# A graph layer kernel: the rows of x turned by DMA from their f16 halves, the combination of x and mean as f16 products, and the masked maximum in passes of 1024 columns

## What is computed

```python
mask = (adj > 0)
deg  = sum(mask, axis=1)
agg  = mask @ x / max(deg, 1)
out0 = relu(concat([x @ W_self + b_self, agg @ W_nb + b_nb]) @ W_comb + b_comb)
x    = layernorm(x + out0)

neib_att = tanh(neigh @ Wn1 + bn1) @ Wn2 + bn2
value    = neigh @ Wv + bv
x_att    = tanh(x @ Wx1 + bx1) @ Wx2 + bx2
ws   = leaky_relu(x_att @ neib_att.T)             # 4096x4096
ws   = softmax(where(adj > 0, ws, -9e15), axis=1)
out1 = concat([x @ Wfx + bfx, ws @ value])
x    = layernorm(x + out1)
```

## Time and profile before

| what | value |
|---|---|
| median of three runs | 768.94 us |
| the profiled execution: its own time | 770.73 us |
| its span | 768.9 us |
| PE busy | 733.2 us (95%) |
| weight loads (PEld) busy | 631.0 us (82%) |
| DVE busy | 610.5 us (79%) |
| ACT busy | 584.7 us (76%) |
| POOL busy | 125.3 us (16%) |
| granted TensorE clock | 0.996 of full |
| DMA issue to landing, mask turn of 128x1024 in bf16 | 4.2 us median |

### The profile page before, as it was taken

One profiled execution on the slowest core, in us unless ns is written; L12 is line 12 of the kernel. 1 busy time (PEld: TensorE's weight loads), 2 busy tenths in 40 slices (PEclk: granted clock), 3 DMA queues, 4 the chain that ended last, 5 costly groups with the idle time before them and its releaser, 6 DMA issues.

```text
span 768.9 us, 20264 instructions
## 1 busy us (share of the span) xinstructions
PE 733.2 (95%) x7536; PEld 631.0 (82%) x7536; DVE 610.5 (79%) x1563; ACT 584.7 (76%) x1078; POOL 125.3 (16%) x241
## 2 busy tenths in 40 slices
PE   5989989999999999999999999999999999999785
PEld 4646768888888888888888889888888888887564
DVE  4886477888888888888888888888888888877874
ACT  2455258888888888888888888888888888888995
POOL 0010120111111111111111111111111111111101
PEclk9999999999999999999999999999999999999999
DMA  8968997876677776676876668677667677620000
GB/s 266 363 151 163 220 246 172 179 173 148 157 150 175 176 180 158 158 156 161 180 179 150 160 164 159 167 180 172 138 171 163 170 179 174 122 43 8 8 9 14
DMA packets 175154, 120.43 MB, mean 157 GB/s; under 512 B 140368, under 2 KB 158672, under 8 KB 175056
## 3 DMA queue, kind: packets, MB, share of 16 engines
q1 hardware_dynamic: 174612, 119.11, 65.1%
q10 hardware_dynamic: 444, 0.02, 0.0%
HBM read 81.35 MB, written 4.19 MB: 111 GB/s over the span
## 4 chain that ended last, share of the span: by engine, by line
PE 87%; ACT 4%; DVE 3%; issue 3%; DMA 1%; POOL 1%; SPq 0%; POOLq 0%; ACTq 0%; DVEq 0%
PE ps_v L1036 20%; PE ps_t L1023 14%; PE ps_agg L999 14%; PE ps_agg L1002 14%; PE ps_agg L1056 7%; PE ps_s L1014 6%; PE ps_v L921 2%; PE ps_s L913 2%; PE ps_x L1073 1%; PE ps_x L1076 1%; ACT score L829 1%; DMA neigh_sb<-in_L_gnn_neigh_dram 1%; ACT score L822 1%; PE ps_x L930 1%; PE ps_t L904 1%
## 5 line engine op out<-in xcount | busy, mean ns | idle before, releaser
L999 PE MATMUL ps_agg<-x,mask_t 128*128 128x257 f16 x1024 | 239.7, 272 | 1.5 <-DMA mask_t<-mask 1.5
L1002 PE MATMUL ps_agg<-x,mask_t 128*128 128x256 f16 x1024 | 234.5, 272 | 0.0
L679 DVE TENSOR_TENSOR late<-ps_t,late 128x512 f16<-128x512 f32 x256 | 174.8, 683 | 74.2 <-ACT late L835 71.6
L1036 PEld LDWEIGHTS ps_v<-v,late 128*128 128x128 f16 x3072 | 189.9, 97 | 50.9 <-DVE late L679 16.6
L1036 PE MATMUL ps_v<-v,late 128*128 128x128 f16 x3072 | 213.5, 219 | 9.2 <-DVE late L679 6.7
L822 ACT ACTIVATE score<-ps_s,sc 128x512 f32<-128x512 f32 x256 | 178.0, 695 | 53.0 <-PE ps_s L1014 51.5
L622 DVE CUSTOM_DVE_ANT_0 score<-score,mask 128x512 f32<-128x512 f32 x256 | 176.2, 688 | 18.7 <-ACT score L822 17.2
L835 ACT CAST late<-ps_t 128x512 f16<-128x512 f32 x256 | 150.2, 587 | 15.2 <-PE ps_t L1023 15.1
L1023 PE MATMUL ps_t<-ident,score 128*128 128x128 f32 x1024 | 157.3, 276 | 3.4 <-ACT score L829 3.4
L829 ACT ACTIVATE score<-score,exp_bias,sc 128x1024 f32<-128x1024 f32 x128 | 158.7, 1240 | 1.6 <-DVE exp_bias L631 1.6
L1023 PEld LDWEIGHTS ps_t<-ident,score 128*128 128x128 f32 x1024 | 107.9, 141 | 6.8 <-ACT score L829 4.7
(11 more groups left out here) (125 smaller groups left out, 705.7 us busy)
## 6 DMA issues: line engine op xcount, KB each, us to landing
adj_sb<-in_adj_dram SPq DMA_DIRECT2D x128, 512.0 KB, 4.7
neigh_sb<-in_L_gnn_neigh_dram SPq DMA_DIRECT2D x8, 512.0 KB, 8.0
score<-in_x_dram SPq DMA_DIRECT2D x8, 512.0 KB, 8.5
x_in<-in_x_dram SPq DMA_DIRECT2D x32, 128.0 KB, 3.9
out_dram<-out_sb SPq DMA_DIRECT2D x32, 128.0 KB, 4.5
mask_t<-mask SPq DMA_TRANSPOSE x128, 4.2
mask<-in_L_gnn_W_comb_dram SPq DMA_DIRECT2D x1, 512.0 KB, 10.1
mask<-in_L_gnn_W_self_dram SPq DMA_DIRECT2D x1, 256.0 KB, 7.1
```

What stands on the lines that cost most here:

```text
L679: dve.tensor_tensor(p_lo[:, k % 2, :], ps_t[k % 2][:, :], p_hi[:, k % 2, :], ALU.subtract).then_inc(p_lo_made, 1)
L999: mm = pe.matmul(agg[:, 0:D + 1], mask_t8[:, c, 0, :], x16[:, c, 0:D + 1], start=(c == 0), stop=(c == NC - 1), skip_group_check=True)
L1002: mm = pe.matmul(agg[:, 0:D], mask_t8[:, c, 0, :], x16[:, c, X_LO:X_LO + D], start=False, stop=False, skip_group_check=True)
L1036: mm = pe.matmul(ps_v[:, 0:DV], p[:, k % 2, chunk], v16[:, c, v:v + DV], start=(c == 0 and part == 0), stop=(c == NC - 1 and part == 2))
```

## The change

The rows of x are no longer turned by PE out of a float32 load. SP turns the 512 columns of f16 halves of a block (`turn_x`, in slot 4 of the block) by a DMA transpose into `x_t`; PE's slot 9 keeps the two transposes of the mean. The turned mean is split: ACT makes the high half (slot 10, 256 columns instead of 512), DVE the low half (`mean_low`, slot 11). `m_both` is scaled and split into `m16` in the preparation (a bound over `m_both`, two more ACT and two more DVE instructions in slots 6 and 7, and a third column in the all-reduce on POOL). The combination is twelve f16 products of 256 columns. Layer 0 scales its input on the way. All stages from the combination on stand one slot later, so the loop has one slot more. The masked maximum goes over 1024 columns at a time, in every second slot, and two quarters of the mask are made one slot later.

```diff
-MASK_SLOTS = (-6, -5, -2, -1)
+MASK_SLOTS = (-6, -4, -2, 0)
 MEAN_AT = 8
 MEAN_T_AT = 9
-MEAN_COPY_AT = 10
-COMBINE_AT = 11
...
+MEAN_SPLIT_AT = 10
+MEAN_LOW_AT = 11
+X_TURN_AT = 4
+COMBINE_AT = 12
...
+            def turn_x(b):
+                sp.wait_ge(x_lo_made, b // TR + 1)
+                at_least(sp, combined, b - 1)
+                sp.dma_start_transpose(x_t[:, b % 2, :, :], x16[:, b, 0:2 * D]).then_inc(x_t_in[b % 2], 16)
...
+            def m_low(c):
+                dve.wait_ge(m_hi_made, c + 1)
+                dve.scalar_tensor_tensor(out=m16[:, 1, c, :], in0=m_both[:, c, :], scalar=m_scale, in1=m16[:, 0, c, :],
+                                         op0=ALU.mult, op1=ALU.subtract).then_inc(m_split, 1)
...
-            def masked_scores(b, k):
-                dve.wait_ge(leaky_made, NG * b + k + 1)
-                dve.wait_ge(mask_made, NQ * b + k // 2 + 1)
-                part = slice(k * GW, (k + 1) * GW)
+            def masked_scores(b, q):
+                dve.wait_ge(leaky_made, NG * b + 2 * q + 2)
+                dve.wait_ge(mask_made, NQ * b + q + 1)
+                part = slice(q * QW, (q + 1) * QW)
...
+            def mean_low(b):
+                dve.wait_ge(mean_hi_made, b + 1)
+                dve.scalar_tensor_tensor(out=mean_t[:, 1, :], in0=ps_agg[b % 2][:, 0:D], scalar=x_scale,
+                                         in1=mean_t[:, 0, :], op0=ALU.mult, op1=ALU.subtract).then_inc(mean_lo_made, 1)
...
-                if d := due(s, SCORE_AT + 1):
-                    masked_scores(*d)
+                if (d := due(s, SCORE_AT + 2)) and d[1] % 2 == 0:
+                    masked_scores(d[0], d[1] // 2)
+                if d := due(s, MEAN_LOW_AT, 0):
+                    mean_low(d[0])
...
-            def mean_x_t_copy(b):
+            def mean_high(b):
...
-                act.copy(mean_x_t[:, :], ps_agg[b % 2][:, :]).then_inc(mean_x_t_copied, 1)
+                act.activation(mean_t[:, 0, :], ps_agg[b % 2][:, 0:D], ACT.Copy, scale=x_scale).then_inc(mean_hi_made, 1)
...
             def mean_transpose(b):
                 pe.wait_ge(mean_made, b + 1)
-                pe.wait_ge(x_in_in[b % 2], 16 * (b // 2 + 1))
                 for dc in range(DC):
-                    pe.transpose(ps_agg[b % 2][:, dc * P:(dc + 1) * P], mean[:, dc * P:(dc + 1) * P], ident[:, :])
-                for dc in range(DC):
-                    mm = pe.transpose(ps_agg[b % 2][:, D + dc * P:D + (dc + 1) * P],
-                                      x_in[:, b % 2, dc * P:(dc + 1) * P], ident[:, :])
...
             def combine(b):
...
+                pe.wait_ge(x_t_in[b % 2], 16 * (b // 2 + 1))
+                pe.wait_ge(mean_lo_made, b + 1)
+                for k, ((r, w), dc) in enumerate(product(HI_LO, range(DC))):
+                    pe.matmul(ps_agg[b % 2][:, 0:D], x_t[:, b % 2, (1 - r) * DC + dc, :], m16[:, w, dc, D:2 * D],
+                              start=(k == 0), stop=False)
+                for k, ((r, w), dc) in enumerate(product(HI_LO, range(DC))):
+                    mm = pe.matmul(ps_agg[b % 2][:, 0:D], mean_t[:, r, dc * P:(dc + 1) * P], m16[:, w, dc, 0:D],
+                                   start=False, stop=(k == 3 * DC - 1))
```

More of the change, by code:

```diff
@@ L48 @@
 RES_BUFS = 4
-MASK_SLOTS = (-6, -5, -2, -1)
+MASK_SLOTS = (-6, -4, -2, 0)
 MEAN_AT = 8
 MEAN_T_AT = 9
-MEAN_COPY_AT = 10
-COMBINE_AT = 11
[L57 to L70, removed]
+MEAN_SPLIT_AT = 10
+MEAN_LOW_AT = 11
+X_TURN_AT = 4
+COMBINE_AT = 12
+LAYER0_AT = 13
+X1_AT = 15
+X1_T_AT = 16
+X1_COPY_AT = 17
+X1_LOW_AT = 18
+HIDDEN_AT = 19
+TANH_AT = 20
+XATT_AT = 21
+STACK_AT = 22
+SCORE_AT = 23
+ROW_MAX_AT = 31
+TURN_AT = 33
+WEIGH_AT = 34
+LAYER1_AT = 42
 SLOTS = NG * (NB - 1) + LAYER1_AT + 1
@@ L146, in gnn_kernel @@
         res = late[:, 1024:2048].rearrange("p (r d) -> p r d", r=RES_BUFS)
+        m_both = late[:, 0:DC * 2 * D].rearrange("p (c d) -> p c d", c=DC)
         x_in = sb("x_in", [P, 2, D], F32)
@@ L149, in gnn_kernel @@
         mean = sb("mean", [P, D], F32)
-        mean_x_t = sb("mean_x_t", [P, 2 * D], F32)
+        mean_t = sb("mean_t", [P, 2, D], F16)
+        x_t = sb("x_t", [P, 2, 2 * DC, P], F16)
         x1 = sb("x1", [P, D], F32)
@@ L205, in gnn_kernel @@
         mask_t_in = [sem(f"mask_t_in{q}") for q in range(NQ)]
+        x_t_in = [sem(f"x_t_in{k}") for k in range(2)]
         x_in_in = [sem(f"x_in_in{k}") for k in range(2)]
@@ L266, in gnn_kernel @@
         mean_made = sem("mean_made")
-        mean_x_t_copied = sem("mean_x_t_copied")
+        mean_hi_made = sem("mean_hi_made")
+        mean_lo_made = sem("mean_lo_made")
+        m_hi_made = sem("m_hi_made")
+        m_split = sem("m_split")
+        m_scaled = sem("m_scaled")
         p_hi_made = sem("p_hi_made")
@@ L606, in first_part @@
                 if s == 3:
-                    x1_weight_bounds()
+                    late_weight_bounds()
                 if s == 5:
-                    scale_x1_weights()
-                if s == 7:
+                    scale_late_weights()
+                if s in (6, 7):
+                    m_low(s - 6)
+                if s == 9:
                     split_fx()
@@ L636, in degrees @@
                 at_least(dve, mean_made, b)
-                dve.tensor_scalar(row[:, 4:5], ps_agg[b % 2][:, X_ONE:X_ONE + 1], EDGE_F8, x_scale, ALU.max,
+                dve.tensor_scalar(row[:, 4:5], ps_agg[b % 2][:, D:D + 1], EDGE_F8, x_scale, ALU.max,
                                   ALU.mult).then_inc(degree_step, 1)
@@ L644, in layer0 @@
                 dve.wait_ge(combined, b + 1)
+                dve.wait_ge(x_in_in[b % 2], 16 * (b // 2 + 1))
                 at_least(dve, x1_made, b)
-                dve.tensor_tensor(l0[:, :], ps_agg[b % 2][:, 0:D], z_bias[:, :], ALU.add).then_inc(l0_step, 1)
+                dve.scalar_tensor_tensor(out=l0[:, :], in0=ps_agg[b % 2][:, 0:D], scalar=l0_inv, in1=z_bias[:, :],
+                                         op0=ALU.mult, op1=ALU.add).then_inc(l0_step, 1)
                 dve.wait_ge(l0_step, base + 1)
@@ L765, in x_high @@
                 part = slice(TR * i, TR * (i + 1))
-                act.activation(x16[:, part, 0:D], x_sb[:, part, :], ACT.Copy, scale=x_scale).then_inc(x_hi_made, 1)
+                act.activation(x16[:, part, X_HI:X_HI + D], x_sb[:, part, :], ACT.Copy, scale=x_scale).then_inc(x_hi_made, 1)
             act.wait_ge(neigh_w_in, 16 * len(NEIGH_WEIGHTS))
@@ L998, in aggregate @@
                         if part == "hi":
-                            mm = pe.matmul(agg[:, 0:D + 1], mask_t8[:, c, 0, :], x16[:, c, 0:D + 1], start=(c == 0),
+                            mm = pe.matmul(agg[:, 0:D + 1], mask_t8[:, c, 0, :], x16[:, c, X_HI:X_ONE + 1], start=(c == 0),
                                            stop=(c == NC - 1), skip_group_check=True)
@@ L1043, in mean_transpose @@
                 pe.wait_ge(mean_made, b + 1)
-                pe.wait_ge(x_in_in[b % 2], 16 * (b // 2 + 1))
                 for dc in range(DC):
-                    pe.transpose(ps_agg[b % 2][:, dc * P:(dc + 1) * P], mean[:, dc * P:(dc + 1) * P], ident[:, :])
-                for dc in range(DC):
-                    mm = pe.transpose(ps_agg[b % 2][:, D + dc * P:D + (dc + 1) * P],
-                                      x_in[:, b % 2, dc * P:(dc + 1) * P], ident[:, :])
-                mm.then_inc(mean_x_t_done, 1)
-            def combine(b):
-                pe.wait_ge(mean_x_t_copied, b + 1)
-                for c in range(2 * DC):
-                    half, dc = divmod(c, DC)
-                    mm = pe.matmul(ps_agg[b % 2][:, 0:D], mean_x_t[:, c * P:(c + 1) * P],
-                                   m_both[:, dc, half * D:(half + 1) * D], start=(c == 0), stop=(c == 2 * DC - 1))
+                    mm = pe.transpose(ps_agg[b % 2][:, dc * P:(dc + 1) * P], mean[:, dc * P:(dc + 1) * P], ident[:, :])
+                mm.then_inc(mean_t_done, 1)
+            def combine(b):
+                if b == 0:
+                    pe.wait_ge(m_split, DC)
+                pe.wait_ge(x_t_in[b % 2], 16 * (b // 2 + 1))
[6 more added lines that the diff above has]
+                                   start=False, stop=(k == 3 * DC - 1))
                 mm.then_inc(combined, 1)
```

53 lines of the change are left out of this document (32 added, 21 removed).

## The result

The changed kernel takes 773.48 us (median of 8 runs, 771.65 to 774.27) beside 768.86 us before (8 runs, 768.70 to 770.57): ratio 1.0054, interval 1.0042 to 1.0066. It is slower, by 0.5%. I had stated 769.6, with 755 to 776. The mechanism that I described is there, step by step; the sizes of the round and of the tail were short, and a stretch at a low TensorE clock was not in the sum.

The account below looks back on a forecast made before the run. PE was taken to bound the loop, not the two-block tail. Profiled 770.73 - 0.3 (loop) + 0 (head) + 1.3 (tail) = 771.7, with the median 1.8 lower, 769.9; stated 769.6 us, range 755 to 776.

Parts of the forecast that it names:

- faster, same and slower: Chances for the whole kernel's time, where same means within 0.3%, 766.6 to 771.2 us: 0.33, 0.31, 0.36.
- PE's gain: Combination with f16 products (0.41 us) and x turns dropped from PE (0.22): 0.63 us a block, 20.2 over 32 blocks.
- The wait that comes: PE idles about 0.62 us ahead of the turn of p in slot 33, waiting for ACT's exponentials behind the mean.
- The round's length: Chain of waits over PE, DVE and ACT from turn of p to the next: 20.96 us summed, 20.88 taken.
- short end: Lower estimate of the round of waits, 20.80 us, which would change the time by -2.4 us.
- rival 2: Round exceeds the old period as wide DVE passes step 1.24 us: 21.14, +6.8 us, 777 with the tail; chance 0.16.
- the first mechanism: The round of waits takes PE's gain in the loop: period 20.88 against 20.89 us, -0.3 us; chance 0.64.
- Head: Preparation and first combinations: added DVE and ACT work against PE's early gain, -1.5 to +1.5 us, taken as 0.
- Tail: End of kernel: one more slot (0 to 2.2 us), later row maxima (0 to 1.6); +1.3 taken, 0 to +3.
- Rival 1: PE stays the bound in the loop, so its whole gain counts: 750 us; chance 0.20 with half-way cases.
- Rival 3: DMA turn of x late, PE waits for x_t at the combination; chance under 0.02, within rival 2's.
- The fixed price of a DVE pass: About 151 cycles per DVE instruction; four passes fewer take 0.63 us of busy time off DVE a block.

Follow-up runs that it names:

- e11: Changed kernel with stages and masks at their old slots, ACT's mean behind p_high and leaky, and 512-column masked maxima; 748.08 us, ratio 0.9731.
- e1: Changed kernel with two lines of ACT's program exchanged, so the exponentials stand ahead of the mean in a slot; 760.03 us, ratio 0.9877.
- e2: Kernel before, with exponentials, turn of p, weighing and layer 1 one slot later, so the exponentials stand behind the mean; 799.37 us, ratio 1.0386.
- e3: Changed kernel with PE computing the scores of group 7 (slot 6) three times, 0.43 us more a block; 773.22 us, ratio 1.0047.
- e4: Changed kernel with PE computing the scores of group 4 (slot 3) three times, 0.43 us more a block; 787.07 us, ratio 1.0225.
- e5: Changed kernel with masked maxima in narrow passes of 512 columns again, ACT's order unchanged; 777.69 us, ratio 1.0110.
- e6: Changed kernel with narrow masked maxima of 512 columns and ACT's exponentials ahead of the mean; 751.38 us, ratio 0.9766.
- e10: Changed kernel with stages and masks at their old slots, wide passes kept, ACT's mean behind p_high and leaky; 752.92 us, ratio 0.9783.
- e9: e1 with the stages from the low half of the mean to the stack one slot earlier, separating layer 0 from wide passes; 751.10 us, ratio 0.9770.

## Why the prediction was right, and where short

The place and the kind of the wait were forecast, and the experiments bear them out. The direction was not: faster, same and slower had 0.33, 0.31 and 0.36. Against the sum, which gave 769.9 before I stated 769.6, the profiles show the loop 3.4 longer (3.14 for -0.3), the head 0.7 shorter and the tail 1.0 longer.

- **PE's gain.** Right: combination 1.30 against 1.31 predicted, 0.63 us a block; e11 shows it whole, period 20.27 against 20.26.
- **The wait that comes.** Right in place, releaser and count: turn of p in slot 33, ACT's exponentials behind the mean, 27 times, 0.67 us for 0.62. e1 removes it by order alone, e2 makes it by order alone, e3 and e4 show which slots of PE lie in the round.
- **The round's length.** Here the sum failed by its size. The rows gave 20.96; I took 20.88, half way to a short end of 20.80, because "the rows lean to the long side". Measured is 20.99: 27 x (20.99 - 20.88) = 3.0 us; the last interval, which lost 0.60 and not 0.11, adds the rest. The mask was indeed shorter (0.60 for 0.69), but layer 0 (1.54 for 1.48) and the first p_low (0.69 for 0.60) were longer, so there was no lean. "It decides from a round of 20.95 on" was right as a point; the cause given for rival 2, wide passes that step by 1.24, was not: they step by 421.22 - 420.07 = 1.15, as taken. The kernel came out on rival 2's side by way of the first mechanism's own steps.
- **Head.** It was taken as 0, within 1.5 either way. Up to slot 33 it is -1.73; PE's gain counts before a block b+3 exists. From 33 to 41 it is +1.07, of which the round explains 0.1; the low clock, at 2.0, more than covers the rest. The sum has no term for the clock. That the two parts nearly cancel, so that the head came out inside its range, is luck: at the full clock the head would have been about 2 us shorter, by an estimate from these 2.0.
- **Tail.** It was taken as +1.3 with 0 to 3; it is +2.28. Both causes that I named are at work. Behind the last aggregation the profiled executions with narrow passes are shorter than their partners with wide ones by 1.4 us (e5, after), 1.9 (e6, e1) and 2.1 (e11, e10), where I had 0 to 1.6. Those without the extra slot are shorter by 2.1 (e10 against e1) and 2.3 (e11 against e6), where I had 0 to 2.2. The other operations give a part of this back, as e11 ends 1.4 sooner there than the kernel before (68.3 against 69.7). These are single profiles.
- **Rival 1** (PE stays the bound, 750) failed here for the reason that I gave, and is what the best version is: 748 to 753 once nothing that PE needs stands behind the mean.
- **Rival 3** (`x_t` late) did not happen: PE waits for `x_t` nowhere in the loop.
- **The fixed price of a DVE pass.** The wide pass takes 1.22 us and the narrow one 0.69; by the rule of the Trainium skill, "VectorE: DVE Perf Modes", section on the TRN2 errata, (elements + 151) cycles at 0.96 GHz, the estimate is 1.22 and 0.69: the traces agree. What this was worth could not be read from the rule: 4.2 us faster where the passes lie in the round (after against e5), 8.6 slower where a wide pass delays p_low, the tail counted in both (e1 against e6).

## What to carry to other kernels

When a change takes work off the engine that is the bound, add up the next round before trusting the gain: follow each engine's queue in program order from the instruction the bound engine waits for, back to itself; if its sum is above the new work per block, that sum is the period. Take the sum as the rows give it, without rounding towards the answer that looks neutral. And on an engine that works in order, put the instruction whose input comes last behind those that others need soon: one such exchange was worth 13 us in one layout and 23 in another.

## What the runs showed of the hardware that I had not expected

GpSimd's adding of the biases (L429) and DVE's wide pass (L653) get in each other's way. In the groups of the kernel after, L429 takes 1581 ns on average; the same instruction takes 745 before and 728 in e9. The timeline after, beside the wide pass that began at 425.29:

```profile
423.90 0.26 POOL L424 TENSOR_SCALAR mv<-mv 128x1 f32<-128x1 f32 x1
425.42 1.67 POOL L429 TENSOR_TENSOR late<-x,bfv_sb 128x256 f32<-128x256 f32 x1 [1.26 <-ACT x L884]
```

GpSimd started second and took 1.67 us. In e1 it started first, kept its 0.73, and DVE took 1.55 in place of 1.22:

```profile
521.07 0.73 POOL L429 TENSOR_TENSOR late<-x,bfv_sb 128x256 f32<-128x256 f32 x1 [0.87 <-ACT x L884]
...
521.32 1.55 DVE L653 CUSTOM_DVE_ANT_0 score<-score,mask 128x1024 f32<-128x1024 f32 x1
```

Whoever came second was held until about the end of the first: GpSimd ended at 427.09, 0.66 us, nearly its undisturbed time, after the end of the pass proper (426.43, where its maximum is read out). In e1 the pass proper ended 1.01 us after GpSimd's 521.80, where 1.15 is its undisturbed step. The Trainium skill, "Trainium Architecture — The Big Picture", section "What this means for kernel authors", says that DVE and GpSimd share a pair of ports to SBUF, as an exclusive lock and not as a split of bandwidth; these two rows agree. In the kernel after it cost nothing that the traces show: the waits of 130 to 690 us have no engine waiting for L429.

Smaller: the pass that scales by a per-row value out of PSUM (L683) takes 0.48 us for 256 columns, where the plain sum in its place took 0.42 before. It is in the round, and it is about what layer 0 was longer (1.54 for 1.48).
